# Graph kernel on one core: the sums of gathered tiles with a 128-column stationary operand, and a gather ring of 8 slots

## The reference

```
h = relu(layernorm(x));  H = gelu(h @ W1.T + b1)
W_tar = gelu(H[src] @ WA.T) @ WB.T                        # 4 mix weights per edge
agg = gelu(segment_sum(H[src][:, :, None] * W_tar[:, None, :], dst))
out_edge = einsum('ehm,em->eh', agg[dst], W_tar)
agg_node = segment_sum(out_edge, dst) / max(count(dst), 1)
out = x + gelu(concat([agg_node, H])) @ W2.T + b2
```

## Time and profile before

| | |
|---|---|
| median of 3 runs | 1301.7 us (1298.65 to 1304.33) |
| the profiled execution's own time | 1304.83 us |
| its span, first to last instruction | 1303.1 us |
| TensorE busy, mean granted clock | 1070.4 us (82%), 0.927 |
| GpSimd busy | 903.8 us (69%) |
| VectorE busy | 947.6 us (73%) |
| ScalarE busy | 604.1 us (46%) |
| stage 0, from the first gather | 160.9 to 286.4 us |
| stages 1, 2, 3, 4 | 286.4 to 451.8, 645.5, 838.3, 1037.5 us |
| stage 5 | 1037.5 to 1223.1 us |

### The profile page before, as it was taken

One profiled execution on the slowest core, in us unless ns is written; L12 is line 12 of the kernel. 1 busy time (PEld: TensorE's weight loads), 2 busy tenths in 40 slices (PEclk: granted clock), 3 DMA queues, 4 the chain that ended last, 5 costly groups with the idle time before them and its releaser, 6 DMA issues.

```text
span 1303.1 us, 25372 instructions
## 1 busy us (share of the span) xinstructions
PE 1070.4 (82%) x7395; PEld 727.5 (56%) x7395; DVE 947.6 (73%) x2601; ACT 604.1 (46%) x1304; POOL 903.8 (69%) x923
## 2 busy tenths in 40 slices
PE   5665127789999989999999999899999997889558
PEld 3454013356767656666666666566666654566324
DVE  7998558888888668888678887578887763532147
ACT  6765664436666445656445655356655200000224
POOL 4766657667777777777777777777777777767037
PEclk9867559989999999999999999999999998999859
DMA  5244552226666655555655555655555567655422
GB/s 206 100 161 190 227 208 56 54 76 169 181 167 175 179 156 164 156 156 156 187 164 157 157 163 159 179 151 156 155 156 152 158 197 163 201 139 161 119 76 83
DMA packets 83891, 201.11 MB, mean 154 GB/s; under 512 B 21917, under 2 KB 33375, under 8 KB 81553
## 3 DMA queue, kind: packets, MB, share of 16 engines
q1 hardware_dynamic: 58282, 142.37, 34.9%
q0 software_dynamic: 25472, 57.11, 18.1%
HBM read 167.18 MB, written 32.22 MB: 153 GB/s over the span
## 4 chain that ended last, share of the span: by engine, by line
PE 46%; DVE 17%; POOL 14%; issue 10%; DMA 7%; ACT 5%; DVEq 2%; SPq 0%; ACTq 0%; POOLq 0%
PE ps L1398 19%; POOL q L664 12%; PE ps L1379 11%; PE ps L1351 10%; DMA q<-node_table,src_g 4%; PE ps L1354 3%; DVE big L1084 2%; PE ps L1403 2%; DVE q L1093 1%; ACT hot_b L800 1%; DVE big L1280 1%; DVE mask L1059 1%; DVE big L1015 1%; DVE big L1029 1%; DVE q L948 1%
## 5 line engine op out<-in xcount | busy, mean ns | idle before, releaser
L664 POOL DMA_INDIRECT q<-node_table,src_g x796 | 770.1, 968 | 273.2 <-issue 216.6
L1398 PE MATMUL ps<-big,q 128*128 128x298 bf16 (+2 forms) x2940 | 464.0, 297 | 0.0
L800 ACT ACTIVATE hot_b<-iota_b,q 128x128 bf16<-128x128 bf16 x847 | 269.7, 389 | 343.8 <-PE ps L1379 343.6
L1351 PE MATMUL ps<-mask,q 128*128 128x96 f32 x1592 | 254.4, 283 | 76.7 <-DVE mask L1059 75.4
L1398 PEld LDWEIGHTS ps<-big,q 128*128 128x128 bf16 x2940 | 264.7, 98 | 82.7 <-issue 2.7
L1093 DVE TENSOR_SCALAR q<-iota_a,q 128x490 bf16<-128x490 f16 (+1 forms) x847 | 269.3, 365 | 24.7 <-issue 12.5
L1379 PE MATMUL ps<-q,hot_b 128*128 128x490 bf16 (+1 forms) x847 | 233.9, 372 | 58.5 <-ACT hot_b L803 25.0
L1351 PEld LDWEIGHTS ps<-mask,q 128*128 128x128 f32 x1592 | 216.7, 194 | 112.2 <-DVE mask L1059 100.7
L1084 DVE TENSOR_TENSOR big<-big,ps 128x490 f32 (+1 forms) x358 | 232.4, 649 | 55.1 <-PE ps L1379 53.8
L1059 DVE TENSOR_TENSOR mask<-eq,q 128x192 f32<-128x192 bf16 x398 | 141.5, 356 | 124.2 <-DMA q<-node_table,src_g 97.0
L1379 PEld LDWEIGHTS ps<-q,hot_b 128*128 128x128 bf16 x847 | 69.9, 97 | 161.4 <-DVE big L1084 61.4
(11 more groups left out here) (134 smaller groups left out, 776.9 us busy)
## 6 DMA issues: line engine op xcount, KB each, us to landing
q<-product_parts SPq DMA_DIRECT2D x245, 388.0 KB
product_parts<-big SPq DMA_DIRECT2D x12, 1552.0 KB, 5.9
q<-node_table,src_g POOLq DMA_INDIRECT x796
node_table<-big SPq DMA_DIRECT2D x12, 280.0 KB, 3.1
own_part<-big SPq DMA_DIRECT2D x12, 256.0 KB, 2.9
big<-own_part SPq DMA_DIRECT2D x3, 1024.0 KB, 10.0
out_dram<-q SPq DMA_DIRECT2D x12, 256.0 KB, 2.0
dense_columns<-q SPq DMA_DIRECT2D x3, 596.0 KB
```

Of the source, the lines that this page charges most:

```text
L664: pool.indirect_dma_start(out=ring[:, t % R, :], out_offset=None, in_=table, in_offset=bass.IndirectOffsetOnAxis(ap=src_g[:, t:t + 1], axi ...
L800: last = nc.scalar.activation(hot_b[:, b % 2, i, :], iota_b[:, :], ACT.Abs, bias=nkey_b[:, t:t + 1])
L1351: nc.tensor.matmul(o[:, 0:MIX * W], ring[:, s + t, 0:D], mask[:, b, t, :, :], start=(t == 0), stop=(t == G - 1))
L1398: last = nc.tensor.matmul(ps[:, 3 + m, 0:n], c[:, LEAD + P * (MIX * part + m):LEAD + P * (MIX * part + m + 1)], counts[k % 2][:, a, c0:c1] ...
```

## The change

The stationary operand of L1354 becomes 128 bf16 columns of the slot: the 13 small ones, the 3 zeros of the table row, and 112 zeros that are written once behind each slot (115 zeros in all). The output is 128 partitions. For that a slot grows from 140 to 196 words (PITCH_R), and GpSimd fills the pads once ahead of the first gather. The ring shrinks from 10 to 8 slots (five groups to four), `eq` from 6 to 4 buffers, and some small tiles move: `iota` (used by the general path alone, which doesn't run on these inputs) and `most_p` into `big`. Since `most_p` then lies where stage 4 reads its counts, its reductions in stage 5 wait until stage 4's units are done. One iota instruction of the prologue goes.

```diff
-R = 10
+R = 8
 ROW = 140
+PITCH_R = 196
-EB = 6
+EB = 4
...
-        ring = q[:, RING0:RING0 + R * ROW].rearrange("p (s d) -> p s d", d=ROW)
-        ring_b = q[:, RING0:RING0 + R * ROW].bitcast(bf16).rearrange("p (s d) -> p s d", d=2 * ROW)
-        KEY0 = RING0 + R * ROW
+        ring = q[:, RING0:RING0 + R * PITCH_R].rearrange("p (s d) -> p s d", d=PITCH_R)
+        ring_b = q[:, RING0:RING0 + R * PITCH_R].bitcast(bf16).rearrange("p (s d) -> p s d", d=2 * PITCH_R)
+        KEY0 = RING0 + R * PITCH_R
...
-        iota = sb("iota", [P, W])
-        most_p = sb("most_p", [P, 1 + NAB])
+        most_p = at(MIX * D0 + 2 * FR, 1 + NAB)
...
+            pool.memset(ring[:, :, ROW:PITCH_R], 0.0).then_inc(ring_padded, 1)
             for t in range(TG):
                 if t >= R and t % G == 0:
                     pool.wait_ge(group_summed, (t - R) // G + 1)
                 pool.indirect_dma_start(
-                    out=ring[:, t % R, :], out_offset=None, in_=table,
+                    out=ring[:, t % R, 0:ROW], out_offset=None, in_=table,
...
                     v.wait_ge(counts_added, CGG)
+                    v.wait_ge(unit_done, NT * (S - 1))
                     nc.vector.tensor_reduce(most_p[:, i:i + 1], counts[1][:, AB * i:AB * i + AB, :], axis=AX.XY,
...
             pe.wait_ge(own_added, NCH)
+            pe.wait_ge(ring_padded, 1)
             for g in range(4):
...
                 for t in range(G):
-                    last = nc.tensor.matmul(o[0:NP, MIX * W:SLOT], ring_b[:, s + t, TP:TP + NP],
+                    last = nc.tensor.matmul(o[:, MIX * W:SLOT], ring_b[:, s + t, TP:TP + P],
                                             eq[:, e, t, :], start=(t == 0), stop=(t == G - 1))
                 last.then_inc(group_summed, 1)
```

More of the change, by code:

```diff
@@ L206, in gnn_kernel @@
         assert MIX * D0 <= HALF and NT * D <= ACC0 - HALF
-        QW = 3104 + R * ROW + CTT + -(-CTT // 2) + HA * NT * CW // 2 + MIX * SW
+        QW = 3104 + R * PITCH_R + CTT + -(-CTT // 2) + HA * NT * CW // 2 + MIX * SW
         q = sb("q", [P, QW])
@@ L239, in gnn_kernel @@
         b1_sb = sb("b1_sb", [P, 1])
-        most_p = sb("most_p", [P, 1 + NAB])
[L241 to L244, removed]
+        single = sb("single", [1, K + 10])
+        smax, marks = single[:, 0:K], single[:, K:K + 8]
+        flag, span = (single[:, K + i:K + i + 1].bitcast(i32) for i in (8, 9))
         done = sb("done", [P, 3])
@@ L301, in gnn_kernel @@
         frow = [big[0:1, MIX * D0 + FR * i:MIX * D0 + FR * (i + 1)] for i in range(2)]
-        assert MIX * D0 + 2 * FR <= HALF
+        most_p = at(MIX * D0 + 2 * FR, 1 + NAB)
+        assert MIX * D0 + 2 * FR + 1 + NAB <= HALF
         acc_g = at(0, PL * NACC).rearrange("p (m n) -> p m n", m=PL)
@@ L313, in gnn_kernel @@
         wide_a = q[0:1, KEY0 + ET:KEY0 + ET + NGG].bitcast(i32)
-        assert GEN0 + 3 * ET + NGG + NGG // 2 <= ACC0 + PL * NA
+        IOTA0 = GEN0 + 3 * ET + NGG + NGG // 2
+        iota = at(IOTA0, W)
+        assert IOTA0 + W <= ACC0 + PL * NA
         idx = src_g[:, 0:U]
@@ L388, in gnn_kernel @@
         eq_ready = sem("eq_ready")
+        ring_padded = sem("ring_padded")
         masks_ready = sem("masks_ready")
@@ L603, in _ @@
                       allow_small_or_imprecise_dtypes=True).then_inc(consts, 1)
-            pool.wait_ge(consts, 4)
+            pool.wait_ge(consts, 3)
             pool.affine_select(out=ident, in_=ident, compare_op=ALU.not_equal, fill=1.0,
@@ L675, in step @@
                             pool.indirect_dma_start(
-                                out=ring[:, s, :], out_offset=None, in_=table,
+                                out=ring[:, s, 0:ROW], out_offset=None, in_=table,
                                 in_offset=bass.IndirectOffsetOnAxis(ap=idx[:, s:s + 1], axis=0),
@@ L756, in _ @@
                 if c == NCH + 2:
-                    act.wait_ge(consts, 7)
+                    act.wait_ge(consts, 6)
                     act.wait_ge(own_ready, NCH)
@@ L1033, in _ @@
             v.wait_ge(early_zeroed, 1)
-            v.wait_ge(consts, 7)
+            v.wait_ge(consts, 6)
             regs_g = [nc.vector.alloc_register(f"start_g{i}") for i in range(6)]
@@ L1199, in _ @@
                                         op=ALU.max).then_inc(cleared, 1)
-                v.wait_ge(cleared, 3)
+                nc.vector.tensor_copy(iota, iota_b[:, 0:W]).then_inc(cleared, 1)
+                v.wait_ge(cleared, 4)
                 nc.vector.tensor_tensor(dloc_a.rearrange("p (j t) -> p j t", t=G),
@@ L1205, in _ @@
                 nc.vector.tensor_copy(base_a, low_a[0:1, :]).then_inc(cleared, 1)
-                v.wait_ge(cleared, 6)
+                v.wait_ge(cleared, 7)
                 nc.vector.tensor_reduce(span[:, :], wide_a, axis=AX.X, op=ALU.max).then_inc(general_ready, 1)
@@ L1244, in _ @@
                         nc.vector.tensor_scalar(base_a, base_a, float(W), float(N), ALU.add, ALU.min).then_inc(moved, 1)
-                        nc.vector.tensor_scalar_add(iota[:, :], iota[:, :], float(W)).then_inc(moved, 1)
+                        nc.vector.tensor_scalar_add(iota, iota, float(W)).then_inc(moved, 1)
                         v.wait_ge(moved, 2 * w + 2)
@@ L1288, in _ @@
         def _(pe):
-            pe.wait_ge(consts, 7)
+            pe.wait_ge(consts, 6)
             pe.wait_ge(ld_w, 80)
```

2 lines of the change are left out of this document (removed).

## The result

| | before | after |
|---|---|---|
| median of 15 runs each, side by side | 1302.25 us (1298.65 to 1310.42) | 1317.56 us (1308.72 to 1323.54) |
| own time of the profiled run, its span | 1304.83, 1303.1 us | 1315.15, 1313.4 us |
| TensorE, GpSimd, VectorE busy | 1070.4, 903.8, 947.6 us | 1021.3, 907.0, 944.0 us |

Ratio 1.0102, 95% interval 1.0085 to 1.0119: slower by 1.0%, some 13 us. The forecast was 1304 us, no change, in a range of 1290 to 1318: the measured time lies clear of the forecast and 0.4 us inside the range. In the two profiles the difference is 10.3 us of span.

What follows compares the result with a forecast made beforehand. GpSimd's gather pace was taken as the bound. Terms -3 - 5 + 7.5 + 2 + 1 = +2.5 us on the profiled 1304.8 gave 1307.3; that run lies 3.1 above the median, so 1304 us, no change; range 1290 to 1318.

Steps and rivals of the forecast that it cites:

- What bounds the kernel: Gathers: GpSimd can't start one more often than every 1.249 us; 796 need 994 us; waits for TensorE hold 29.7 us.
- TensorE per group: Gaps around the 13-column matmuls (L1354): 0.17 us saved per group, 0.14 on average, 56 us over 398 groups.
- What of it arrives: Part of TensorE's 56 us that shortens the kernel: -5 us in stages 1 to 4, -3 in stage 0.
- Ring of four groups: GpSimd stops one group earlier at hold-ups: 3 x 2.5 = +7.5 us (0 to +10); jitter in stages 1 to 4: +2.
- the three places: Hold-ups costing 2.5 us each: end of stage 0, the landing that took 9.0 us, and `check_bounds`.
- Four `eq` buffers: VectorE's next `eq` waits for the group two back, a sum it awaits anyway behind the mask: 0 us (0 to +3).
- The added wait: Ahead of L1151, first reduction moves to about 1036.5, mask behind it to 1039.6: +1 us (0 to +3).
- The pads: Fill on GpSimd ahead of the first gather: about 1.1 us, hidden by stage 0's full ring; +1 without that cover.
- Slower: the ring becomes the bound: Stages 2 and 4: turn-around of 10.4 us makes groups take 2.6 us, +15, stage 5 +5: 1318 us; chance 0.21.
- The signs: GpSimd's waits grow in number, hardly in stages 1 to 4; those end a few us earlier; stage 5 takes 3 to 7 longer.
- Faster: Rival: TensorE's relief arrives and the ring isn't missed, waits of stage 5 shrink too: -13 us, 1289 us; chance 0.22.
- The change doesn't do what it says: Rival: way in stays 0.21 us, loads take 0.10 each, TensorE loses 24 us: about 1320 us; chance 0.07.

Runs made afterwards that it cites:

- operand-alone kernel: Kernel before with only the 128-column operand, every second bf16 cell, 145-word rows; ten slots, six eq buffers, no pads or added wait: 1297.91 against 1304.64 us, 0.9952.
- the five kernels: Profiled: before; wide operand alone, ten slots; the same, eight slots; changed; changed without added wait. Spans 1303.1, 1296.6, 1309.5, 1313.4, 1321.2 us.
- the eight-slot kernel: The operand-alone kernel with a ring of eight slots instead of ten, six eq buffers, no pads, no added wait: 1317.30 against 1301.71 us, 1.0120.

## Why the prediction was right or wrong

The forecast itself, no change at 1304 us, missed by 13 us. The range held the measured time by 0.4 us at its upper end, which is luck more than aim: the end stood for another mechanism (below). One term of the sum carries the miss.

**What bounds the kernel: right.** GpSimd's pace of 1.249 us, not TensorE with its 46% of the chain. Taking 48 us of busy time from TensorE (1070.4 to 1022.7 in the operand-alone kernel) moved the median by 0.5%. The floor, with all 29.7 us of waits gone, was not reached: the lowest time of any run is 1296.83. (By the trace seven units follow the last group's sum, not six; nothing hangs on it.)

**TensorE per group: right in size.** 0.17 us was forecast where both gaps go, and 0.18 is what the starts show (0.205 to 0.112 on the way in, 0.137 to 0.054 behind the first small matmul). That the way out saves nothing where a second group's f32 load follows at once was wrong: over the 129 groups of that kind it went from 0.134 to 0.054 as well. So the average of 0.14 was low, and yet busy time fell by less than its 56 us, by 49.1: the start of one instruction and busy time aren't the same measure. The Trainium skill (TensorEngine Tiling, Key Properties) says that a change of tiling mode drains TensorE. The rows before and after agree with a drain around the 13-column form; that this form is such a mode, no run shows. Its other rule (TensorE: Matmul & The Clock Gate, LDWEIGHTS: a load takes its columns at 1.2 GHz) didn't decide: the load's record grew from 87 to 114 ns, but the next work starts 0.06 us behind the pair's first matmul.

**What of it arrives: right in size, its split less so.** -3 - 5 = -8 was forecast, and the operand alone gave -6.3 us (0.9952). By stage, in GpSimd's waits: stages 1 to 4, where all 5.1 us were counted, gave 3.3. Stage 0, counted at 3, gave 0.9. The other 2.0 of the 6.5 us between the two profiles are in the last column, which moves by 5.6 over the five kernels.

**Ring of four groups: this step failed, by its size.** "3 x 2.5 = +7.5" and "jitter +2 (0 to +8)" make 9.5; the runs showed 22 (1.0120 against 0.9952, 18 to 26). In the two profiles it is 12.9 of span, of which 11.7 are waits: 3.5 in stage 0, 2.5 in stages 1 to 4, 5.4 in stage 5. That is hardly over my terms. Of the three places two were right; the one in stage 0 is where the ring first fills, not the stage's end. The other 9 us aren't in these two traces. Six are the distance from the profiled run of the eight-slot kernel (1311.29) to its median (1317.30), and some 3 are that the kernel before took 1304.64 us beside the one and 1301.71 beside the other. Even with the jitter at its upper end the terms make 15.5, and with both at their upper ends 18, where the measured cost only begins. So the price that one profile of before gives for a buffer was too low here by about half. Where in a median run the rest is spent no trace shows.

**Four `eq` buffers: right for this measurement.** At 0 (0 to +3): on A the kernel with four (1.0097) isn't slower than that with six (1.0120), both with eight slots and the wide operand. L1048 waits 12.3 us for TensorE there, in 9 places. On B the same edit alone cost 0.7%, and there `make_eq`, which waits for the sum of two groups back, waits 145.8 us. That this wait is the cause of the 0.7% is argued only.

**The added wait: right.** +1 forecast; 0.9 us in GpSimd's waits, nothing that the medians tell. The places were right as well: the reduction at 1036.52 (1036.5 forecast), the mask at 1039.50 (1039.6). **The pads:** the fill takes 0.47 us, not 1.1, and is too small to see: the first gather starts at 161.2 instead of 161.0, and over the five kernels of the table between 159.7 and 161.7.

**The rivals.** "Slower: the ring becomes the bound", priced at 1318, met the measured 1317.6, but through another place. (Its terms, +15 and +5 on 1301.7, make 1322.) It was to come from groups that turn around in over 10 us all through stages 2 and 4. Waits of stages 1 to 4 are 5.5 us in the profile of after, as much as before (5.1), with one gather per 1.268 us there (1.271 before). In that profile the cost is at the two ends. The signs: GpSimd's waits grew in time, from 29.7 to 37.7 us, but not in number (85 to 78), and stage 4 ended 3.1 us later, not a few earlier; stage 5 took 5.0 us longer, inside the 3 to 7 named. "Faster" fell: even with ten slots only 6 to 7 of its 13 us came. "The change doesn't do what it says" fell by the timeline.

So: of an expected gain of 8 us 6.3 came, and two slots of the ring of ten were given away for it, which cost 22, where 9.5 were expected. Still open are the split of the 22 us in a median run, the part of the 596 KB load in stage 5, and why three of four chips take 16 to 18% longer.

## What to carry to other kernels

When the chain names one engine and another runs within 2% of its least pace, look at the second's waits before you count on a gain: here they held 29.7 us, and 48 us less work on the first engine brought 6. Don't pay for a faster engine with buffers of the bounding one, and don't price such a buffer from one profile: here a pair of profiles gave 12.9 us and the medians some 20. And a wide operand needn't be padded: finite neighbours behind a stride do as well as zeros, if the outputs they make are left unread.

## What the runs showed of the hardware

- A bf16 operand that takes every second cell costs the same as a contiguous one: TensorE busy 1022.7 us against 1021.3, mean load 115 ns against 114.
- TensorE stood idle for 3.50 us in the changed kernel (1036.40 to 1039.90), its granted clock at 1.00 up to there. Then the clock averages 0.56 from 1039.9 to 1043.1, so most of that stretch is at the lower of its two levels, and a 400-column matmul shows 0.49 us (above) where it shows 0.33 at the full one.
- Around two bf16 matmuls with 13 stationary columns TensorE lost 0.09 us on the way in and 0.08 on the way out against the same pair with 128, in the medians of 398 groups.
- Chips differ by 16 to 18% on the same kernel (1302 to 1305 us on one, 1507 to 1531 on three). GpSimd's, VectorE's and ScalarE's single operations take as long; TensorE's show 1 to 6% more, and the rest is waits. The chips also rank two edits differently (four `eq` buffers instead of six: 0.7% on B, no cost seen on A).
